# Loading the first context and value-weight chunk ahead of the token rows in a cross-attention and expert kernel

## What is computed

```python
x = x + fake_quant(layernorm(x)) @ fake_quant(ctx)           # layer 0, attention's place
x = x + moe(layernorm(x))                                    # 16 routed experts (top 2 of 2 groups) + 2 shared
q, k, v = layernorm(x) @ Wq.T, ctx @ Wk.T, ctx @ Wv.T        # layer 1: 32 query heads, 8 key/value heads of 128
x = x + softmax(rmsnorm(q) @ rmsnorm(k).T * scale + mask) @ v @ Wo.T
x = x + gated_low_rank_experts(layernorm(x))                 # 64 experts of rank 8, top 16
```

## Time and profile before

| what | us |
|---|---|
| median of three runs | 670.56 |
| lowest and highest of them | 669.53, 681.09 |
| the profiled execution, its own time | 670.89 |
| its span in the profile | 669.1 |

### The profile page before, as it was taken

The page is one execution under the profiler, slowest core; times in us unless marked ns, Lnnn a source line. Parts: engine busy times, 40 slices in busy tenths (PEclk is TensorE's granted clock), DMA queues, the critical chain, the costliest instruction groups (busy, mean ns, idle before and its releaser), DMA issues.

```text
span 669.1 us, 11221 instructions
## 1 busy us (share of the span) xinstructions
PE 628.0 (94%) x3012; PEld 280.4 (42%) x3012; DVE 420.8 (63%) x980; ACT 351.9 (53%) x764; POOL 339.0 (51%) x329
## 2 busy tenths in 40 slices
PE   2999699999999999999997899999999979999997
PEld 1445243444444444444442244444444424444453
DVE  6898977244443337455556999999999940000773
ACT  4375445243333323776667677777777743133132
POOL 5992245355555432487877444444444424368011
PEclk9999899899999999999999899999999989999999
DMA  9902245644444331179776999999999993324001
GB/s 344 365 0 80 48 90 98 176 128 125 133 135 146 118 139 67 62 175 211 173 166 156 200 172 174 187 181 182 181 185 181 181 186 131 127 82 169 1 1 64
DMA packets 200314, 95.65 MB, mean 143 GB/s; under 512 B 187962, under 2 KB 188090, under 8 KB 197341
## 3 DMA queue, kind: packets, MB, share of 16 engines
q1 hardware_dynamic: 197778, 91.02, 56.5%
q10 hardware_dynamic: 2507, 4.27, 2.1%
HBM read 48.03 MB, written 1.09 MB: 73 GB/s over the span
## 4 chain that ended last, share of the span: by engine, by line
PE 66%; DVE 11%; issue 8%; POOL 7%; ACT 3%; SPq 2%; DMA 1%; POOLq 0%; DVEq 0%; ACTq 0%
PE ps L282 22%; PE ps L283 21%; PE ps L284 21%; POOL wsp L1092 4%; POOL hlr L1092 3%; SPq L378 2%; DVE st L1221 1%; DMA stage<-in_first_chunks 1%; PE ps L405 1%; DVE f32r L1403 1%; PE ps L652 1%; DVE x_sb L1311 1%; DVE f32r L1247 1%; DVE hlr L1482 1%; DMA pT<-hlr 0%
## 5 line engine op out<-in xcount | busy, mean ns | idle before, releaser
L1092 POOL TENSOR_TENSOR wsp<-stage,wsp 128x512 f16<-128x512 f32 (+1 forms) x93 | 135.2, 1477 | 127.1 <-ACT wsp L950 59.4
L970 ACT ACTIVATE f32r<-f32r,mneg 128x512 f32<-128x512 f32 x128 | 91.5, 715 | 29.7 <-DVE mneg L1472 29.7
L1092 POOL TENSOR_TENSOR hlr<-f32r,hlr 128x512 f16<-128x512 f32 x52 | 60.3, 1168 | 88.4 <-ACT hlr L878 54.9
L1472 DVE CUSTOM_DVE_ANT_0 f32r<-ps,nmask 128x512 f32<-128x512 f32 x128 | 82.5, 680 | 1.9
L1178 POOL TENSOR_SCALAR hlr<-f32r,rinv 128x512 f16<-128x512 f32 x64 | 43.5, 692 | 47.1 <-DVE rinv L1477 46.9
L282 PE MATMUL ps<-q_sb 128*128 128x512 f16 x128 | 50.5, 394 | 17.9 <-POOL q_sb L1092 11.9
L1178 POOL TENSOR_SCALAR stage<-f32r,rinv 128x512 f16<-128x512 f32 x64 | 43.5, 692 | 46.3 <-DVE rinv L1477 46.3
L1390 DVE TENSOR_REDUCE ss<-f32r 128x4 f32<-128x512 f32 x48 | 32.8, 685 | 47.8 <-ACT f32r L866 47.7
L282 PE MATMUL ps<-k_sb,q_sb 128*128 (+1 forms) x128 | 49.7, 389 | 8.9 <-DVE mneg L1472 6.5
L282 PE MATMUL ps<-xT,wsp 128*128 128x512 f16 x144 | 55.7, 387 | 0.0
L283 PE MATMUL ps<-xT,wsp 128*128 128x512 f16 x144 | 55.6, 386 | 0.0
(11 more groups left out here) (242 smaller groups left out, 1350.1 us busy)
## 6 DMA issues: line engine op xcount, KB each, us to landing
stage<-in_moe SPq DMA_DIRECT2D x18, 512.0 KB, 3.7
stage<-in_wq SPq DMA_DIRECT2D x8, 1024.0 KB, 5.0
stage<-in_wo SPq DMA_DIRECT2D x8, 1024.0 KB, 5.1
stage<-in_moe SPq DMA_DIRECT2D x18, 256.0 KB, 3.2
pT<-gates_dram ACTq DMA_DIRECT2D x16, 256.0 KB, 3.1
k_sb<-in_wkv SPq DMA_DIRECT2D x3, 1024.0 KB, 18.8
stage<-in_first_chunks SPq DMA_DIRECT2D x4, 512.0 KB, 7.5
q_sb<-in_ctx_nat SPq DMA_DIRECT2D x1, 2048.0 KB, 14.8
```

What stands on the lines that cost most here:

```text
L970: act.activation(f32r[:, j % 4, :], f32r[:, j % 4, :], ACT.Exp, bias=mneg[:, j % 4:j % 4 + 1], scale=-1.0, accum_out=psum_col[:, j % 4:j % ...
L1092: return pool.tensor_tensor(dst_lo, src, dst_hi, ALU.subtract)
L1472: dve.tensor_tensor_reduce(f32r[:, j % 4, :], ps[j % 4][:, :], nmask[:, qt, :], 0.125, BIG, ALU.add, ALU.min, mneg[:, j % 4:j % 4 + 1]).th ...
```

## The change

The first of the four chunks is issued ahead of the token rows; the other three keep their place. No instruction of a compute engine is added, removed or moved, and no wait is changed.

```diff
             sp.dma_start(par[:, 0:PAR_SC + 4], params).then_inc(s_par, 16)
+            def first_chunk(c):
+                sp.dma_start(stage[:, :, c * GW:(c + 1) * GW], first_chunks[c]).then_inc(s_first[c], 16)
+
+            first_chunk(0)
             sp.dma_start(x_sb[:, :, :], x_rows.rearrange("(t p) d -> p t d", p=P)).then_inc(s_x, 16)
-            for c in range(KC):
-                sp.dma_start(stage[:, :, c * GW:(c + 1) * GW], first_chunks[c]).then_inc(s_first[c], 16)
+            for c in range(1, KC):
+                first_chunk(c)
             sp.dma_start(kv_land[:, 0, :], ctx_t).then_inc(s_ctx, 16)
```

## The result

The changed kernel takes 672.23 us in the median of 22 runs (670.09 to 677.87), the kernel before 670.13 us in the median of 22 runs beside it (668.86 to 681.09). The ratio is 1.0032, with a 95% interval of 1.0020 to 1.0044: 2.1 us slower. That is within 2% and inside the predicted range (668.6 to 672.7), but on the wrong side; the forecast was 0.5 us faster. The profiled execution took 671.73 us with a span of 670.0.

A forecast was written before the change was run, and what follows sets the result against it. TensorE, busy 628.0 of 669.1 us, was taken as the bound for most of the program, but not throughout the opening. From 670.89 us, a shift of minus 0.85 to 0, taken as minus 0.5, gave 670.4 us; range 668.6 to 672.7.

The forecast's parts named there:

- When the two land: Opening loads: first chunk lands 2.7 us earlier, token rows 1.35 us later, second chunk and later loads don't move.
- GpSimd gains 0.85 us: GpSimd's opening subtractions: third starts at 10.83 instead of 11.72, so its last piece ends about 53.5 instead of 54.34.
- The wait that appears: TensorE before batch 1: idle 2.3 us for VectorE's rounding, starting at 24.6 instead of 24.98, leaving 0.35 us won.
- The clock: TensorE in batch 1: the idle stretch halves its clock, costing 1.7 us, bounds 0 and 3.4.
- The cover: VectorE's chain before the L405 transposes follows GpSimd's end, ready 0.85 us earlier; TensorE gains 0.85 or, after a clock fall, nothing.
- The sum: Whole kernel: minus 0.85 to 0 us against 670.89, taken as minus 0.5, giving 670.4 us.
- the clock makes it slower: Rival, batch 1: a slow stretch of 6.8 us costs 3.4 us, total 672.6 us; chance 0.15.
- The token rows' delay is carried through VectorE: Rival, after the rounding: VectorE's slack fails and all comes 1.35 us later, 672.2 us; chance 0.08.
- The full gain arrives: Rival: TensorE's start 2.7 us earlier moves all work behind it, 668.2 us; chance 0.06.
- does not do what it says: Rival, opening loads: both transfers share the DMA engines and nothing moves, 670.9 us; chance 0.08.

The follow-up runs named there:

- The mask's run: Kernel before with the 512 KB mask moved ahead of the token rows, chunks kept behind the tokens: 672.76 us, 1.0034.
- second profile: Changed kernel run and profiled once more with no edit: 671.92 us, 1.0027 against the kernel before.
- first profile: Profiled execution of the changed kernel in the main measurement, no further edit: 671.73 us.
- the halved chunk: Changed kernel with the early chunk issued as two transfers of 256 KB: 673.73 us, 1.0061 against the kernel before.
- the pause between the issues: Changed kernel with SyncE issuing the second chunk and all later loads only once the first chunk has landed: 671.88 us, 1.0033 against the kernel before.
- the pieces of 8 KB: Changed kernel with token rows in landing order, 128 pieces of 8 KB instead of 512 of 2 KB: 672.42 us, 1.0040 against the kernel before.
- the pause of GpSimd: GpSimd's last two opening pieces held until normalised tokens are copied out of PSUM: kernel before 668.81 us, 0.9973; changed kernel 672.65 us, 1.0027.
- The clamp at 28.55: From the kernel before with only VectorE's token work held until the third chunk landed, transfers in old order: 678.70 us, 1.0130.

## Why the prediction was wrong

*When the two land.* This is the step that failed. "The token rows land 1.35 us later" measured 3.7 and 2.9; "the second chunk and all later loads ... don't move" measured +2.2 and +1.4; "the first chunk lands 2.7 us earlier" measured 1.9. The prediction read the pace of a running queue, 1.35 us for each chunk, and used it for the queue's first transfers, where two things differ. The rate is lower while the token rows move (244 and 292 against 392 GB/s), and the 16 shares drift apart, so that the last is 2.2 and 1.6 us behind the first. The mask's run shows that this isn't a matter of the chunk. Why the rate is low and what makes the shares drift is not settled: neither the later issues, nor the size of the pieces, nor one transfer in place of two explains the drift. (The 436 GB/s that the prediction names from the Trainium skill stand in that section for loads issued by GpSimd; these are issued by SyncE. No term rests on them.)

*GpSimd gains 0.85 us.* Wrong by the same error: with the second chunk late it had two pieces done early and then stood idle, and it ended 1.4 us later in the one profile and 0.6 in the other (54.98).

*The wait that appears.* Right in kind and place; 3.6 us and not 2.3. The rounding ended at 26.92 and not at 24.6, and TensorE was ready for it at 23.4 and not at 22.3 (22.6 in the second profile). Batch 1 began 2.0 and 1.2 us later, not 0.35 earlier.

*The clock.* The price of 1.7 us for a stretch of 3.4 was right in four of the five profiles in which it fell in batch 1: in the first one token transposes stood at 39.04 against 35.34, that is 2.0 for the start and 1.7 for the clock. With the halved chunk it was 2.6. But it did not fall in the second profile after a wait of the same 3.6 us, nor after 2.2 us with the pause between the issues, and it did fall after 2.1 us with the pieces of 8 KB. Whether it falls is not set by the length of the wait alone.

*The cover.* Right for the kernel before, as the pause of GpSimd shows: VectorE's chain went at GpSimd's pace, and 1.33 us of TensorE's lateness were free. The two bounds give the measured places. In the first profile TensorE decides: 3.7 late less 1.33 is 2.4, measured 2.2. In the second, VectorE's chain decides: 0.65 late at L1240, measured 0.64 at the transposes. Neither profile has the gain that the forecast counted on, because GpSimd ended later and not 0.85 us earlier.

*The sum.* That the measured +2.1 us lies near the first profile's 2.2 at the transposes is partly luck: the second has 0.6 there, and at the end of the first pair of profiles only 0.9 is left (spans of 670.0 and 669.1). After the transposes the clock stood at half for 24 us in the profile before and for 14 us in the changed one. The executions differ in both, so the median is not the shift of one trace. And the forecast, wrong on when the tokens land, was off by only 1.8 us of 670 because the cover took up part of the lateness.

*The rivals.* The slower one, "the clock makes it slower", came near to the time (672.6) for another reason: its stretch was 3.4 us and not 6.8; the lateness of the start did the rest. (The trace before has a fourth fall that the prediction does not count, at 78.91, and it is a long one.) "The token rows' delay is carried through VectorE" gives 672.2, the measured time, and that is luck: the delay was 2.9 and 3.7 us and not 1.35, and in the first profile VectorE's chain, 1.65 late at L1244, was not what ended last. "The full gain arrives" and "does not do what it says" fell.

## What to carry to other kernels

In the first microseconds of this program a transfer moved ahead of another cost that one more than its bytes: the last of 16 shares decides, and the shares drifted apart. So look at when the last share of each transfer lands, and not at the pace alone. Before giving one engine an earlier start, find the next place at which it waits for the engine that pays; here both led into one wait for the rounding. And where small steps of VectorE last ten times as long beside GpSimd's pieces (1.73 us against 0.17), try to hold back the pieces that nobody needs yet: one line of that kind gained 1.8 us in the kernel before, where the reordered load lost 2.1.

## What the runs showed that was not expected

VectorE does not always get its turn beside GpSimd. The Trainium skill ("SBUF — State Buffer", section "SBUF: two separate sides") has a lock that whichever starts first holds for one instruction. If the waiting engine always had the next turn, which the section does not say, a step would lose at most one piece, here about 1.1 us. The clamp at 28.55 lost nine microseconds against GpSimd's pieces in a row, so the trace disagrees with that reading. Elsewhere the turns do change: in the kernel before, the twelve subtractions from 30.76 on took 1.43 us each beside VectorE's work, and not 1.12. No run shows what decides between the two.

The 16 shares of the token rows lay 1.4 to 3.0 us apart in the eight profiles in which 512 KB stood ahead of them on the queue, and the transfers behind them kept that spread up to 17 us (less closely with the pause between the issues). In the five profiles with the token rows first they lay 0.5 to 1.1 us apart.
